# AdaLN and a quantised feed-forward layer: the first stage put in another order, the sums of the last two pairs too, and products of zeros ahead of the gates

## What is computed

```
q_emb = relu(cond @ W3 + b3)                      # 64 batches, 512 gates each
z     = relu(((64*x + sum_over_sequence(x)) * q_emb) @ W2 + b2)
w_up, w_down = (code - 7.5) * scale               # 4-bit codes, a scale for each 64 columns
y1    = z @ w_up.T + b_up + z @ lora_a @ lora_b   # 512 -> 2048
out   = x + relu(y1) @ w_down.T + b_down + relu(y1) @ lora_a' @ lora_b'
```

## Time and profile before

| | us |
|---|---|
| median of 3 runs (lowest, highest) | 765.02 (764.61, 765.81) |
| the profiled execution | 765.55 |
| its span, first to last instruction | 763.7 |

### The profile page before, as it was taken

How to read it: one execution, slowest core, us unless ns; L and a number is a source line. 1 busy time by engine, 2 the same in 40 slices (tenths; PEclk the granted TensorE clock), 3 DMA queues, 4 the chain that set the end, 5 groups by cost and what they waited for, 6 DMA issues and landing times. The chain is left out here.

```text
span 763.7 us, 9568 instructions
## 1 busy us (share of the span) xinstructions
PE 740.0 (97%) x3248; PEld 609.5 (80%) x3248; DVE 554.5 (73%) x725; ACT 420.4 (55%) x727; POOL 78.3 (10%) x68
## 2 busy tenths in 40 slices
PE   6599999999999999999999999999999999999997
PEld 5478888878878878888888888888888888888876
DVE  6598866776976487767776877767776877757585
ACT  3866175574754175666647265666656363626531
POOL 0063524333430000000000000000000000000000
PEclk9899999999999999999999999999999999999999
DMA  8957978988628696655516798766515696665552
GB/s 325 308 185 218 292 214 264 288 262 250 221 99 290 210 383 230 220 194 193 180 56 229 254 385 265 222 202 192 180 56 183 229 382 220 199 192 194 193 165 111
DMA packets 92160, 170.60 MB, mean 223 GB/s; under 512 B 8528, under 2 KB 25040, under 8 KB 91472
## 3 DMA queue, kind: packets, MB, share of 16 engines
q1 hardware_dynamic: 91824, 169.90, 67.4%
q10 hardware_dynamic: 288, 0.08, 0.0%
HBM read 130.10 MB, written 40.89 MB: 224 GB/s over the span
## 5 line engine op out<-in xcount | busy, mean ns | idle before, releaser
L1138 PE MATMUL ps<-x_hi,ring 128*128 128x512 f32 x672 | 262.1, 390 | 3.0 <-DVE x_lo L932 1.8
L1139 PE MATMUL ps<-x_lo,ring 128*128 128x512 f32 x672 | 261.5, 389 | 0.0
L1140 PE MATMUL ps<-x_hi,ring 128*128 128x512 f32 x672 | 261.4, 389 | 0.0
L1138 PEld LDWEIGHTS ps<-x_hi,ring 128*128 128x128 f32 x672 | 126.1, 188 | 31.4 <-DVE x_lo L932 2.7
L1140 PEld LDWEIGHTS ps<-x_hi,ring 128*128 128x128 f32 x672 | 126.1, 188 | 26.3
L1139 PEld LDWEIGHTS ps<-x_lo,ring 128*128 128x128 f32 x672 | 126.1, 188 | 26.1
L388 ACT ACTIVATE xt<-xt,gated,gate_n 128x64 f32<-128x64 f32 x216 | 74.6, 430 | 37.2 <-DVE gated L741 37.2
L497 ACT ACTIVATE f<-ps,bias 128x512 f32<-128x512 f32 x96 | 64.8, 690 | 42.2 <-PE ps L1140 42.2
L932 DVE TENSOR_TENSOR x_lo<-x_sum,x_hi 128x512 fp32r<-128x512 f32 x96 | 76.8, 818 | 4.2 <-ACT x_hi L535 3.4
L853 DVE TENSOR_TENSOR ps<-s,ps 128x512 f32<-128x512 f32 x48 | 33.3, 693 | 51.1 <-PE ps L1140 50.7
L890 DVE TENSOR_TENSOR res<-ps,res 128x512 f32<-128x512 f32 x72 | 48.3, 687 | 23.6 <-PE ps L1140 23.2
(11 more groups left out here) (80 smaller groups left out, 1002.0 us busy)
## 6 DMA issues: line engine op xcount, KB each, us to landing
ring<-made_w SPq DMA_DIRECT2D x336, 256.0 KB, 3.7
made_w<-made SPq DMA_DIRECT2D x16, 1280.0 KB, 6.0
xt<-in_x SPq DMA_DIRECT2D x32, 256.0 KB, 5.6
code<-in_codes SPq DMA_DIRECT2D x16, 512.0 KB, 8.3
scale<-made_s SPq DMA_DIRECT2D x16, 512.0 KB, 8.0
res<-in_x SPq DMA_DIRECT2D x4, 2048.0 KB, 10.1
made_w<-plain SPq DMA_DIRECT2D x64, 128.0 KB, 6.3
out<-res SPq DMA_DIRECT2D x12, 512.0 KB, 5.5
```

The costliest lines, as they stand in the source:

```text
L1138: pe.matmul(dest, w_hi, a_hi, start=start, stop=False, skip_group_check=True)
L1139: pe.matmul(dest, w_hi, a_lo, start=False, stop=False, skip_group_check=True)
L1140: return pe.matmul(dest, w_lo, a_hi, start=False, stop=stop, skip_group_check=True)
```

## The change

Nothing of what is computed changes. In SP's list W3 comes in two parts (the columns of gate 0 first), all of x0 to x4 goes ahead of the copy of the scales, that copy is cut in two (units 0 and 1 first, the other 14 later), the low-rank tables lose the unused fourth quadrant (96 partitions in place of 128) and are cut in two as well, and the four loads of W2 go to ACT's queue. POOL zeroes a tile of 128 by 192, and TensorE does seven products of 64 columns with it ahead of the gates; their result is never read. Tile 1 is modulated by ACT and tile 6 by DVE, where it was the other way round. The first three W2 steps of half 0 go pass by pass, each pass with its own wait. `low_rank(0)` goes from after step (1, 0) to after step (1, 1). The last unit's tail does M6 first in its own bank, while ACT copies M1's bank to `s4` and DVE adds that to the result.

The sums of pairs 6 and 7 in superblock 3 are taken alternately. DVE's order from unit 12 to unit 14 is now: totals 6.0, 7.0 / (additions to the result) / totals 6.1, 7.1, lows 6.0, 7.0 / totals 6.2, 7.2, low 6.1 / share / lows 7.1, 6.2 / low 7.2, totals 6.3, 7.3 / lows 6.3, 7.3 / share / lows 6.4, 7.4 (pair.step). It was: totals 6.0, 6.1 / totals 6.2, 6.3, low 6.0 / lows 6.1, 6.2 / share / totals 7.0, 7.1, low 6.3 / low 6.4, total 7.2, low 7.0 / low 7.1 / share / total 7.3, lows 7.2, 7.3 / low 7.4. ACT's `x2_high` go in the same new order. `share` is the subtraction for M3's bank (line 853).

```diff
-    ON_DVE, ON_ACT = (0, 1, 2, 3, 5), (4, 6, 7)
+    ON_DVE, ON_ACT, SUMMED = (0, 2, 3, 5, 6), (1, 4, 7), (0, 1, 2, 3, 4, 5, 7, 6)
+
+    def sum_no(s, t):
+        return SUMMED.index(t) + 1 if s == 0 else 8 * s + t + 1
...
-        raw_w3 = sb("raw_w3", [P, KC, D], F32, "x2", 8192)
+        raw_w3 = sb("raw_w3", [P, KD, KC, P], F32, "x2", 8192)
+        warm = sb("warm", [P, 3 * SEQ], F32, "f")
...
-            sp.dma_start(raw_w3[:], w3[:]).then_inc(cond_loaded, 16)
-            for k in range(KD):
-                load_x(0, k)
-                sp.dma_start(raw_w2[:, k, :], w2[:, k, :]).then_inc(w2_raw[k], 16)
-                if k == 1:
-                    sp.dma_start(made_s, scales.unsqueeze(2).to_broadcast([UNITS, 2, COPIES, 1024])).then_inc(scales_copied, 16)
-            sp.dma_start(raw_tables[:], tables[:]).then_inc(tables_loaded, 16)
-            load_x(0, KD)
-            load_x(0, KD + 1)
+            sp.dma_start(raw_w3[:, 0], w3[:, 0]).then_inc(cond_loaded, 16)
+            load_x(0, 0)
+            sp.dma_start(raw_w3[:, 1:KD], w3[:, 1:KD]).then_inc(w3_loaded, 16)
+            for t in range(1, 5):
+                load_x(0, t)
+            copy_scales(slice(0, 2), first_scales_copied)
+            sp.dma_start(raw_tables[0:THREE, 0:2 * D + T], tables[:, 0:2 * D + T]).then_inc(tables_loaded, 16)
+            load_x(0, 5)
+            load_x(0, 7)
             load_codes(0)
+            load_x(0, 6)
+            sp.wait_ge(first_scales_copied, 16)
+            load_scale(0)
+            load_codes(1)
+            load_scale(1)
+            copy_scales(slice(2, UNITS), scales_copied)
+            sp.dma_start(raw_tables[0:THREE, 2 * D + T:], tables[:, 2 * D + T:]).then_inc(rest_loaded, 16)
+            load_codes(2)
             sp.wait_ge(scales_copied, 16)
-            load_scale(0)
-            load_x(0, KD + 2)
-            load_x(0, KD + 3)
-            for u in (1, 2):
-                load_codes(u)
-                load_scale(u)
+            load_scale(2)
             sp.wait_ge(w2_split, KD)
...
             s = SBS - 1
             for dd in range(2):
-                for t, (a, j) in enumerate(((1, 0), (0, 1), (0, 0), (1, 1))):
...
 
             act.dma_start(raw_cond[:], cond[:]).then_inc(cond_loaded, 16)
-            act.dma_start(bias[:, 0:biases.shape[1]], biases[:]).then_inc(bias_loaded, 16)
+            for k in range(KD):
+                act.dma_start(raw_w2[:, k, :], w2[:, k, :]).then_inc(w2_raw[k], 16)
+                if k == 0:
+                    act.dma_start(bias[:, 0:biases.shape[1]], biases[:]).then_inc(bias_loaded, 16)
             act.wait_ge(bias_loaded, 16)
             act.activation(b_spare, b3[:, 0:1], ACT.Relu).then_inc(bias_done, 1)
-            w2_high(0)
-            for k in range(KD):
+
+            def gate_tile(k):
                 act.wait_ge(gate_ready, k + 1)
                 act.activation(gate[:, k, :], ps[4 + k][:, 0:BATCH], ACT.Relu, bias=b3[:, k:k + 1]).then_inc(gate_done, 1)
+
+            gate_tile(0)
+            w2_high(0)
             x_high(0, 0)
-            w2_high(1)
+            for k in range(1, KD):
+                gate_tile(k)
             act.wait_ge(gate_done, KD)
             act.mul(gate_n[:], gate[:], float(SEQ)).then_inc(gate_done, 1)
+            w2_high(1)
+            x_modulate(0, 1)
             x_high(0, 1)
             w2_high(2)
             x_high(0, 2)
             w2_high(3)
             x_high(0, 3)
-            act.wait_ge(tables_loaded, 16)
-            act.copy(lora[:].rearrange("p v d -> p (v d)"), raw_tables[:, 0:2 * D]).then_inc(tab_cast, 1)
-            act.copy(wide_flat[:, 0:T], raw_wide[:, 0:T]).then_inc(tab_cast, 1)
             x_modulate(0, 4)
             x_high(0, 4)
-            x_modulate(0, 6)
+            act.wait_ge(tables_loaded, 16)
+            act.wait_ge(warmed, 1)
+            act.copy(lora_flat, raw_lora).then_inc(tab_cast, 1)
             z_tile(0, 0, 0, 0)
             z_tile(0, 0, 1, 1)
-            x1p_high(0, 0)
             x_high(0, 5)
+            act.copy(wide_flat[:, 0:T], raw_wide[:, 0:T]).then_inc(tab_cast, 1)
+            x_modulate(0, 7)
+            x_high(0, 6)
             z_tile(0, 0, 2, 2)
             z_tile(0, 0, 3, 3)
+            x_high(0, 7)
+            x1p_high(0, 0)
             x1p_high(0, 2)
-            x_high(0, 6)
-            x_modulate(0, 7)
-            x_high(0, 7)
-            act.copy(wide_flat[:, T:], raw_wide[:, T:]).then_inc(tab_cast, 1)
             plain_high(0)
             for m in range(KD):
                 z_tile(0, 1, m, (4 + m) % RING6)
                 if m % 2:
                     x1p_high(1, m - 1)
+            act.wait_ge(rest_loaded, 16)
+            act.copy(wide_flat[:, T:], raw_wide[:, T:]).then_inc(tab_cast, 1)
 
 
...
                         x_high(s + 1, {8: 0, 10: 2}[n])
                         x_high(s + 1, {8: 1, 10: 3}[n])
                     before = (s, n)
-            pass_c11(*before)
+
+            act.wait_ge(prod[M1], chain_no(SBS - 1, LAST[-1]) + 1)
+            act.copy(s4[:], ps[4 * (before[1] % 2) + BP][:]).then_inc(q_down_done, 1)
 
         @block.gpsimd
         def _(pool):
+            pool.memset(warm[:], 0.0).then_inc(zeroed, 1)
             for u in range(UNITS):
                 w = whole[u % 3][:].rearrange("p (i q a c) -> p i q a c", i=2, q=2, a=2)
...
 
             def lora_low():
...
             x_modulate(0)
+            x_sum(0, 1)
             w2_low(0)
-            x_sum(0, 1)
-            x_shift(1)
             x_low(0, 0)
-            x_modulate(1)
-            w2_low(1)
+            x_gate(0, 1)
             x_sum(0, 2)
             x_shift(2)
-            x_low(0, 1)
             x_modulate(2)
-            w2_low(2)
+            w2_low(1)
             x_sum(0, 3)
             x_shift(3)
+            x_low(0, 1)
+            x_modulate(3)
+            w2_low(2)
             x_low(0, 2)
-            x_modulate(3)
-            w2_low(3)
             x_sum(0, 4)
             x_gate(0, 4)
+            w2_low(3)
             x_low(0, 3)
-            lora_low()
-            wide_low(slice(0, T), 2)
             x_sum(0, 5)
             x_shift(5)
             x_modulate(5)
-            x_sum(0, 6)
-            x_gate(0, 6)
+            x_low(0, 4)
             x_sum(0, 7)
             x_gate(0, 7)
+            lora_low()
+            x_low(0, 5)
+            x_sum(0, 6)
+            x_shift(6)
+            x_modulate(6)
+            wide_low(slice(0, T), 2)
+            x_low(0, 6)
             dequantize(0)
-            x_low(0, 4)
+            x_low(0, 7)
             add_lora(0)
-            x_low(0, 5)
             x1p_low(0, 0)
             x1p_low(0, 2)
-            x_low(0, 6)
+            plain_low(0)
             dequantize(1)
-            x_low(0, 7)
-            plain_low(0)
             dve.wait_ge(bias_loaded, 16)
             dve.scalar_tensor_tensor(out=b_c22, in0=b_down[:, 2:4], scalar=2.0, in1=b_down[:, 0:2], op0=ALU.mult,
                                      op1=ALU.subtract).then_inc(bias_done, 1)
-            wide_low(slice(T, NH * P), 3)
             add_lora(1)
             x1p_low(1, 0)
             x1p_low(1, 2)
+            wide_low(slice(T, NH * P), 3)
 
 
...
+            dve.wait_ge(q_down_done, down_no(SBS - 1, 3, 1) - 8 + 1)
+            dve.wait_ge(res_summed, 4 * (SBS - 2) + 4)
+            dve.tensor_tensor(to, to, s4[:], ALU.add).then_inc(res_summed, 1)
+            dve.wait_ge(res_summed, 4 * (SBS - 2) + 5)
+            add_res(*before, BQ)
             add_res(*before, BP)
-            add_res(*before, BQ)
 
         @block.tensor
...
 
+                if s == 0 and j == 0 and k < KD - 1:
+                    passes = ((x_hi_done, w2_cast, w2_in_ring[k][:, 0], xm_hi[:, k, :]),
+                              (x_hi_done, w2_split, w2_in_ring[k][:, 1], xm_hi[:, k, :]),
+                              (x_split, w2_split, w2_in_ring[k][:, 0], xt_lo[:, j, k, :]))
+                    for n, (x_ready, w_ready, still, moving) in enumerate(passes):
+                        pe.wait_ge(x_ready, k + 1)
+                        pe.wait_ge(w_ready, k + 1)
+                        for m in range(KD):
+                            mm = pe.matmul(ps[bank_of(m)][:], still[:, m * P:(m + 1) * P], moving, start=k == 0 and n == 0,
+                                           stop=False, skip_group_check=True)
+                    mm.then_inc(w_step, 1)
+                    return
                 pe.wait_ge(x_split, 8 * s + 4 * j + k + 1)
...
 
+
+            pe.wait_ge(zeroed, 1)
+            for n in range(7):
+                mm = pe.matmul(ps[3][:, 0:SEQ], warm[:, 0:P], warm[:, P:P + SEQ], start=True, stop=True)
+            mm.then_inc(warmed, 1)
             pe.wait_ge(cond_loaded, 32)
             for m in range(KD):
+                if m == 1:
+                    pe.wait_ge(w3_loaded, 16)
                 for k in range(KC):
```

(62 more changed lines are left out.)

40 lines of the change are left out of this document (23 added, 17 removed).

## The result

| | before | changed |
|---|---|---|
| median (lowest, highest) | 764.86 (764.61, 765.81), 4 runs | 753.02 (751.26, 753.24), 4 runs |
| the profiled execution | 765.55 | 751.26 |
| its span | 763.7 | 749.5 |

The ratio is 0.9838, interval 0.9821 to 0.9855: 12 us less.

A forecast was written before the change was run, and what follows sets the result against it. TensorE, 97% busy, bounds the kernel, losing time only in the first 50 and last 30 us. 765.55 - 13.2 + 0.7 + 0.4 + 1.2 - 3.3 = 751.4; run median 750.9, plus 1 gives 752.0; range 748 to 757.5.

The forecast's parts named there:

- The end: Last units: three TensorE waits for low parts and ACT's copy go, none takes their place; 3.3 us.
- The first plain unit: First stage: DVE's list from x0's landing sets TensorE's first plain unit at 36.4 us instead of 49.66; gain 13.2 us.
- rival 1: Two load queues take from each other, x1 to x3 and biases 1 to 3 us late; 753.5 to 756; chance 0.15.
- The durations of DVE's list beside POOL: First stage: two `x1p_low` take 3.99 us and `plain_low` 1.75 while POOL forms sums.
- Zeros lift no clock: Ahead of the gates: seven zero products don't raise TensorE's clock; cost 0 to 1.4 us, taken 0.1.
- The clock ahead of the first plain unit: TensorE's 2.6 us stand before the first plain unit may bring the low clock; cost 0 to 2, taken 0.7 us.
- `x1p_low` for the second half: First plain unit's second half: the other `x1p_low` pair ends at 42.9 us, needed at 42.5; cost 0.4 us.
- The stores behind the tables' wait: Unit 0's stores, issued after SP's wait, land at 57.5 us, delaying ACT and unit 1's ReLUs; 0 to 2.5, taken 1.2.
- the 1 us that I allowed for unfound waits: Whole kernel: 1 us added to 750.9 for waits not found in three hand-merged lists, giving 752.0.
- Rival 2: Plain units can't follow the earlier start; TensorE waits 4 to 7 us in several; 755.5 to 758.5; chance 0.14.
- rival 3: First stage gives nothing back, chain order not the cause; only the end gains; 761.7 us; chance 0.04.
- rival 4: First scales' copy holds SP, so scales come 3.2 us late: 755; slower only past 40.6 us; chance beyond that 0.03.

The follow-up runs named there:

- one queue: The changed kernel with W2's four loads back in SP's list, each behind the x tile of its number: 753.17 us, ratio 0.9841 to before.
- POOL late: The kernel of stores first (zeros kept), with POOL's first weight sums only after `plain_low(0)`: 749.02 us, ratio 0.9781 to before.
- stores first: The changed kernel with SP issuing plain unit 0's stores ahead of its wait for the tables and the `res` load: 750.45 us, ratio 0.9803 to before.
- old loads: The changed kernel's compute lists with the loads in the order of before, all on SP's queue: 759.83 us, ratio 0.9927 to before.

## Why the prediction was right, point by point

The median is 753.02 for 752.0 forecast, within the range, and the mechanism is in the main the one forecast: DVE's list sets the first plain unit. Where that list starts to count was taken wrongly, and one of the prediction's own signs of being wrong came true: it allowed 3 us of TensorE's waits between the first plain unit and 235 us, and the profiles have 3.2 and 4.6 (1.7 before). That the total still came within 1 us is in part luck, as the terms show.

- **The end**, 3.3 us: measured alone 3.7. The three waits went and none replaced them.
- **The first plain unit**, 36.4 us: 37.27 and 37.64. Two errors partly cancelled. The loads were mis-sized: x0 at 6.15 and 7.04 for 5.0, the biases at 8.16 and 8.51 for 6.3. The rest of W3 landed at 7.98 and 8.34; the prediction names no time for it, and its gates follow one another from 4.4 as if it were there by 5.3. So the first W2 record came at 10.56 and 10.92 for 8.05, and `x_gate(0, 1)` at 11.19 and 11.54 for about 9.4 (x1 at 7.5 and the three operations up to it). That is rival 1's late landing, at 2 us, though by W3 and not by x1. That "all of it is one queue from the landing of x0" was the wrong starting point: by the profiles above, the rest of W3 set it. Behind `x_gate(0, 1)` the list took 26.1 us for about 27.0, with `x1p_low` at 3.46 for 3.99 and waits of 0.3 for 0.8. The Trainium skill ("DMA: Bandwidth & Descriptors", "Issuing engines are not separate DMA queues") says that transfers of several issuers share the same DMA engines. The runs agree: a second queue only moved the landings about. Against one queue x0 came 1.2 and 2.1 us later (6.15 and 7.04 for 4.99) and the rest of W3 1.3 and 0.9 us earlier (7.98 and 8.34 for 9.24), and the time was the same (752.95 for 753.17).
- **The durations of DVE's list beside POOL**: `plain_low` 1.75 as taken, `x1p_low` 0.5 us less than taken. POOL late shows that POOL's sums lengthen them: 5.20 us for three instructions beside POOL (3.45 + 1.75), 3.57 alone.
- **Zeros lift no clock**: right by both profiles without them. That they would cost next to nothing (0.1) was forecast, and holds with the stores first; in the changed kernel as it stands leaving them out gives 2 us, by the stores' wait, which nothing in the prediction foresaw.
- **The clock ahead of the first plain unit**, 0.7 us: nothing. TensorE waited 1.48 us, not 2.6, since its own part was later by the same loads, and the records behind came 0.23 us apart. The term itself was not wrong: with the old loads the wait was 1.73 us and the low pace came, for about 1.6 us.
- **`x1p_low` for the second half**, 0.4 us: 0.73 and a restart (0.07 longer to the next start).
- **The stores behind the tables' wait**, 1.2 us: the mechanism was right to the instruction (57.5 us forecast for ACT's release, 56.7 and 57.9 measured), the size too small for the median. From the first plain unit to the W2 product that waits for a ReLU in superblock 1's second half (223.67 before, 213.43 and 215.34 after) the changed kernel lost 2.1 us in the one profile and 3.7 in the other, for 2.3 forecast in all. Stores first gives 2.5 of them back. This is the term of the sum that was mis-sized most, by 1.3 us; the 1 us that I allowed for unfound waits covered it, and since that allowance named no wait, this is luck.
- **Rivals 2, 3 and 4.** Rival 2's mechanism came in part: waits in the plain units cost up to 3.7 us, just under its 4 to 7, by ACT held for the stores. Without the end the change gave 8.7 us, so rival 3 fell. The first scales' copy released SP at 14.18, against 13.2 taken, and `dequantize(0)` did not wait.

## What to carry to other kernels

When a matrix engine waits on a chain of elementwise work, add up that engine's own list, and start the sum at the last landing that it needs, not at the first: here the list of 30 us gave the new start within 1.3 us, with two errors that partly cancelled, and the landing that counted, that of the rest of W3, was one that the sum didn't hold. It does so only while the loads stay ahead of the list; with the old order of loads the start was 45.0. Then look at which waits an earlier start brings forward in the other queues: a transfer parked behind a semaphore on SP cost 2.5 of some 15 us, and swapping two lines gave it back. Loads and lists moved the first plain unit by 4.2 and 4.7 us alone and by 12.0 together, so neither should be judged without the other.
